# Quantizing two chunks at once, and a reciprocal with Sqrt in place of Ln and Exp, in a fused attention and FP4 feed-forward kernel

## What is computed

```python
xn = _layernorm(x, axis=-1)                      # (x - m) / sqrt(v + 1e-5)
x = x + attention(xn, Wqkv, bqkv, Wproj, bproj, mapping) + ffn(xn, w_gate, w_up, w_down)

def fp4_quant_dequant(x):                        # blocks of 16 along the last dimension
    scale = max(|xb|) / 6.0, at least 1e-12
    idx = searchsorted([0.25, 0.75, 1.25, 1.75, 2.5, 3.5, 5.0], |xb / scale|)
    q = [0, 0.5, 1, 1.5, 2, 3, 4, 6][idx] * sign(xb) * scale

def ffn(x, w_gate, w_up, w_down):                # H = 1024, I = 2816
    gate = fp4_linear(x, w_gate)                 # both operands quantized
    y = fp4_linear(x, w_up)
    h = silu(gate) * y
    return fp4_linear(h, w_down)                 # h is quantized as well
```

## Time and profile before

| | |
|---|---|
| median of 3 runs | 6398.97 us (6398.97 to 6400.04) |
| time of the profiled execution | 6415.45 us |
| span of its slowest core (core 6) | 6413.9 us |
| spans of the 8 cores | 6352.1 to 6413.9 us |
| VectorE busy | 4122.6 us, 64% of the span |
| TensorE busy | 2353.3 us, 37% |
| ScalarE busy | 616.3 us, 10% |
| GpSimd busy | 184.6 us, 3% |

### The profile page before, as it was taken

How to read it: one execution, slowest core, us unless ns; L and a number is a source line. 1 busy time by engine, 2 the same in 40 slices (tenths; PEclk the granted TensorE clock), 3 DMA queues, 4 the chain that set the end, 5 groups by cost and what they waited for, 6 DMA issues and landing times.

```text
span 6413.9 us, 41448 instructions; the slowest of 8 cores (6352.1 to 6413.9 us)
## 1 busy us (share of the span) xinstructions
PE 2353.3 (37%) x12222; PEld 1121.9 (17%) x12373; DVE 4122.6 (64%) x6313; ACT 616.3 (10%) x1270; POOL 184.6 (3%) x249
## 2 busy tenths in 40 slices
PE   2664566646200000002434343434343343433343
PEld 0223422233000000000211111111111111111111
DVE  4882368732799999997565656464646465656565
ACT  0222212221000000000000000000000000000000
POOL 0001100011000000000000000000000000000000
PEclk9775577756555555555656565656666666666666
DMA  4211132112200000000000000000000000000000
GB/s 76 69 59 51 55 118 69 61 45 89 72 29 27 26 26 26 27 24 16 12 9 17 9 17 9 17 9 17 8 17 8 17 8 17 8 17 8 17 8 12
DMA packets 86070, 196.80 MB, mean 31 GB/s; under 512 B 42295, under 2 KB 42311, under 8 KB 85847
## 3 DMA queue, kind: packets, MB, share of 16 engines
q0 software_dynamic: 26544, 100.74, 5.1%
q1 hardware_dynamic: 59304, 93.42, 4.8%
HBM read 135.41 MB, written 67.12 MB: 32 GB/s over the span
## 4 chain that ended last, share of the span: by engine, by line
DVE 30%; PE 10%; issue 7%; DMA 4%; ACT 2%; DVEq 1%; SPq 0%; ACTq 0%; POOLq 0%; POOL 0%
PE psA L926 6%; DVE sc L69 6%; DVE sc L65 6%; DMA sc<-partial_dram 2%; DVE sc L58 2%; DVE sc L60 2%; DVE sc L76 2%; DVE bstats L51 2%; DVE sc L991 2%; DVE sc L71 2%; PE psQ L943 2%; PE psT L917 1%; ACT hqT L961 1%; DMA out<-sc 1%; DVE sc L62 1%
## 5 line engine op out<-in xcount | busy, mean ns | idle before, releaser
L65 DVE SCALAR_TENSOR_TENSOR sc<-sc 128x512 f32<-128x512 f32 (+3 forms) x876 | 734.1, 838 | 94.7 <-DVE sc L65 2.3
L69 DVE SCALAR_TENSOR_TENSOR sc<-sc 128x512 f32<-128x512 f32 (+3 forms) x876 | 734.1, 838 | 93.3 <-DVE sc L69 1.8
L825 PE MATMUL psT<-ident,wq_bf 128*128 128x128 bf16 x528 | 67.1, 307 | 1260.7 <-DVE wq_bf L78 1260.7
L917 PE MATMUL psT<-ident,hq 128*128 128x128 bf16 x704 | 90.3, 306 | 1041.4 <-DVE hq L78 961.5
L982 DVE TENSOR_TENSOR sc<-psA,sc 128x512 f32<-128x512 f32 x32 | 22.1, 692 | 610.8 <-PE psA L926 610.8
L926 PE MATMUL psA<-wdqT,hqT 128*128 128x512 bf16 x1376 | 381.3, 448 | 45.3 <-ACT hqT L961 45.3
L991 DVE TENSOR_TENSOR sc<-sl,psU 128x512 f32<-128x512 f32 x96 | 65.6, 683 | 485.5 <-ACT sl L971 485.5
L825 PEld LDWEIGHTS psT<-ident,wq_bf 128*128 128x128 bf16 x528 | 51.0, 138 | 1276.9 <-issue 1276.9
L60 DVE TENSOR_TENSOR sc<-sc 128x512 f32<-128x512 f32 (+3 forms) x292 | 244.7, 838 | 31.4 <-DVE sc L58 1.4
L71 DVE SCALAR_TENSOR_TENSOR sc<-sc 128x512 f32<-128x512 f32 (+3 forms) x292 | 244.7, 838 | 31.1 <-DVE sc L69 0.9
L76 DVE TENSOR_TENSOR sc<-sc 128x512 f32<-128x512 f32 (+3 forms) x292 | 244.7, 838 | 30.8 <-DVE sc L74 0.5
(11 more groups left out here) (161 smaller groups left out, 4483.1 us busy)
## 6 DMA issues: line engine op xcount, KB each, us to landing
sc<-xin SPq DMA_DIRECT2D x64, 512.0 KB
qkv_dram<-qkv_tile POOLq DMA_DIRECT2D x32, 768.0 KB, 3.6
partial_dram<-sc POOLq DMA_DIRECT2D x32, 512.0 KB, 3.4
sc<-partial_dram SPq DMA_DIRECT2D x32, 512.0 KB
out<-sc POOLq DMA_DIRECT2D x32, 512.0 KB, 2.9
wrow<-wg SPq DMA_DIRECT2D x22, 512.0 KB
wrow<-wu SPq DMA_DIRECT2D x22, 512.0 KB
xqT_dram<-xqTst POOLq DMA_DIRECT2D x32, 256.0 KB, 4.4
```

The lines of the kernel that those rows point to most:

```text
L65: sv.inc(vec.scalar_tensor_tensor(L[:, 0:n], a2[:, 0:n], c, L[:, 0:n], ALU.is_gt, ALU.add))
L69: sv.inc(vec.scalar_tensor_tensor(S[:, 0:n], a2[:, 0:n], c, S[:, 0:n], ALU.is_gt, ALU.add))
L917: m = tensor.transpose(psT[:, 128 * c:128 * (c + 1)], hq2[:, (gt - 1) % 2, 128 * (8 * g + c):128 * (8 * g + c + 1)], ident[:])
```

## The change

Two independent edits.

In the layer-norm stage VectorE computes the reciprocal of variance + 1e-5 itself, and ScalarE takes its square root with one activation in place of two. VectorE's instructions per tile become 26 and ScalarE's 9, and the counts are moved accordingly.

In the FFN stage VectorE takes the six chunks in three pairs. It multiplies both chunks of a pair, side by side into `sc2`, and then quantizes them with one call of `_emit_quant` over 1024 columns (768 for the last pair). The instructions per tile fall from 122 to 65. `hmultv` now names the two multiplies at the head of a pair; the waits of TensorE and ScalarE on it are written as before.

```diff
                     def cva(t):
-                        return svA + 25 * t
+                        return svA + 26 * t
 
                     def csa(t):
-                        return ssA + (10 * t - 8 if t >= 1 else 0)
+                        return ssA + (9 * t - 8 if t >= 1 else 0)
...
                                 sv.inc(vec.tensor_scalar_add(stats[:, 14:15], stats[:, 13:14], 1e-5))
+                                vec.wait_ge(sv.h, sv.v)
+                                sv.inc(vec.reciprocal(stats[:, 15:16], stats[:, 14:15]))
                                 vec.wait_ge(ss.h, rstdv(t))
...
-                                    scal.wait_ge(sv.h, cva(t) + 4)
-                                    ss.inc(scal.activation(stats[:, 15:16], stats[:, 14:15], AF.Ln))
-                                    scal.wait_ge(ss.h, ss.v)
-                                    ss.inc(scal.activation(stats[:, 14:15], stats[:, 15:16], AF.Exp, scale=-0.5))
+                                    scal.wait_ge(sv.h, cva(t) + 5)
+                                    ss.inc(scal.activation(stats[:, 14:15], stats[:, 15:16], AF.Sqrt))
...
             def cvf(gt):
-                return svD + (122 * gt - 2 if gt >= 1 else 0)
+                return svD + (65 * gt - 2 if gt >= 1 else 0)
...
             def hmultv(gt, ci):
-                return cvf(gt) + (2 if gt >= 1 else 0) + 20 * ci + 1
+                pq, k = ci // 2, ci % 2
+                return cvf(gt) + (2 if gt >= 1 else 0) + 21 * pq + k + 1
 
             def quantdonev(gt):
-                return hmultv(gt, 5) + 19
+                return cvf(gt) + (2 if gt >= 1 else 0) + 63
...
-                                for ci, (i0, iw) in enumerate(nic_chunks):
-                                    vec.wait_ge(ss.h, siluv(gt, ci))
-                                    ub = psU if ci % 2 == 0 else psB
-                                    uoff = 0 if ci % 2 == 0 else 512
-                                    sv.inc(vec.tensor_tensor(sc2[:, 0:iw],
-                                                             sl[:, 512 * (ci % 2):512 * (ci % 2) + iw],
-                                                             ub[:, uoff:uoff + iw], ALU.mult))
-                                    _emit_quant(vec, sc2[:, 0:iw], iw // 16, bstats,
+                                for pq in range(3):
+                                    pw = 0
+                                    for k in range(2):
+                                        ci = 2 * pq + k
+                                        i0, iw = nic_chunks[ci]
+                                        vec.wait_ge(ss.h, siluv(gt, ci))
+                                        ub = psU if ci % 2 == 0 else psB
+                                        uoff = 0 if ci % 2 == 0 else 512
+                                        sv.inc(vec.tensor_tensor(sc2[:, pw:pw + iw],
+                                                                 sl[:, 512 * (ci % 2):512 * (ci % 2) + iw],
+                                                                 ub[:, uoff:uoff + iw], ALU.mult))
+                                        pw += iw
+                                    _emit_quant(vec, sc2[:, 0:pw], pw // 16, bstats,
                                                 sc3, sc4, sc5, sc6,
-                                                hq2[:, gt % 2, i0:i0 + iw], sv)
+                                                hq2[:, gt % 2, nic_chunks[2 * pq][0]:nic_chunks[2 * pq][0] + pw], sv)
```

More of the change, by code:

```diff
@@ L354, in sc_off @@
                     def sc_off(t):
-                        return 2 if t <= T - 1 else 0
-                    rstdv = lambda t: csa(t) + 2
+                        return 1 if t <= T - 1 else 0
+                    rstdv = lambda t: csa(t) + 1
                     xnTev = lambda tm1: csa(tm1 + 1) + sc_off(tm1 + 1) + 1
@@ L372, in _ @@
                                 if t >= 2:
-                                    sync.wait_ge(sv.h, cva(t - 2) + 5)
+                                    sync.wait_ge(sv.h, cva(t - 2) + 6)
                                 sync.dma_start(out=xbA[t % 2][:],
@@ L440, in _ @@
                                 if t <= T - 1:
-                                    vwait = cva(t) + 6
+                                    vwait = cva(t) + 7
                                     tensor.wait_ge(sv.h, vwait)
```

## The result

The changed kernel takes 6046.72 us (median of 9 runs, 6037.54 to 6143.07), the kernel before 6399.5 us (10 runs, 6385.18 to 6416.46). The ratio is 0.9448, with a 95% interval of 0.9432 to 0.9465: 353 us faster. The forecast was 6082 us with a range of 6048 to 6122.

A forecast was written before the change was run, and what follows sets the result against it. The prediction took VectorE's quantization on a serial FFN tile loop as the bound: 9.86 us a tile, 316 us over 32, plus 1 us of layer norm, off 6415.45, less 16.5 to the median, gives 6082 us, range 6048 to 6122.

The forecast's parts named there:

- What bounds the kernel: FFN stage: each tile is one serial loop of about 108 us, with VectorE's 72 us of quantization on it full length.
- The price of a call: FFN quantization: 4.2 us a call whatever its width, about 0.22 us an instruction, so each merged pair saves 4.2 us.
- Rival (c): FFN quantization: wide instructions each take twice a narrow one, only gaps are saved; 26 us gain, 6372 us; chance 0.02.
- The rule of 58 cycles of fixed cost: FFN quantization: 60 ns saved for each of 57 instructions, 0.8 us a tile, about 6373 us; the sum went by the rows.
- The new wait: First pair of each FFN tile: second multiply waits for chunk 1's silu, 3.73 us plus 0.10; no cost in later pairs.
- The old stretch: VectorE's FFN tile before: five periods of 12.67 us plus a last chunk of 8.63 us, 71.98 us in all.
- The two gaps at no change: FFN loop: down matmuls, store, load and first gate keep their instructions and order, so no change in cost.
- rival (b): FFN loop: TensorE pieces drift to slow kind, 6178 us, or fast kind, near 6000 us; chance 0.04 each.
- The layer-norm part: Layer-norm stage: one ScalarE step out, a VectorE reciprocal in; between -6 and +2 us, taken as -1 us in all.
- Slower (rival d): FFN pairs 1 and 2: banks come back only after the pair's quantization; +330 us, 6729 us; chance 0.02.

The follow-up runs named there:

- e5: Changed kernel with 8 idle multiplies of 1024 columns a tile put in front of the second pair's quantization; 6426.09 us, ratio 0.9994 to the kernel before.
- e7: Changed kernel, but a tile's load waits for the store of the tile two before it, not the last one; 5696.42 us, ratio 0.8885.
- e12: Changed kernel with the earlier load, the next tile's first four chunks ahead of transposes and down matmuls, adds behind the second pair; 4976.55 us, ratio 0.7753.
- e10: Kernel before, with each quantization of 512 columns done as two of 256; 7124.57 us, ratio 1.1082.
- e2: Kernel before with only the layer-norm edit (reciprocal and Sqrt); 6388.81 us, ratio 1.0006.
- e4: Changed kernel, but TensorE and ScalarE take a pair's banks back only when its quantization has ended; one run, 6643.68 us.
- e9: Changed kernel unaltered, timed again beside the kernel before on another chip; 6085.61 us against 6431.02, ratio 0.9461.

## Why the prediction was wrong by 36 us

The mechanism held; what failed are sizes. Two terms of the sum were mis-sized, the wait for the second silu (3.83 us taken, 3.51 measured) and the old stretch (71.98 us taken, 72.28 measured), and the last step, from the profiled slowest core to the median, carried one core's distance from the others over as if it were fixed. Term by term:

- **What bounds the kernel** held: one serial loop a tile, VectorE's stretch on it one to one. e5 put the length back and lost all of the gain; e7 and e12 took the gaps away as the chain of waits had them.
- **The price of a call**, 4.2 us beside its elements, taken from another stage, held (19.66 us again, 1225 ns again), and e10 confirmed it at a third width with 4.4. Rival (c) falls with the 1225 ns: the wide instructions kept their price in this stage. The rule of 58 cycles of fixed cost in the Trainium skill, VectorE: DVE Perf Modes, section on the TRN2 errata, is decided against by measurement: 0.22 us an instruction with the gap, where 60 ns would give 5.7 us a tile in e10 and 22.1 came. The prediction left out that the same section calls this row too low itself and puts the fixed part near 150 cycles; the 159 ns of the earlier trace rows agree with that.
- **The new wait** was there, once a tile, and nowhere else. Its size is the first term that was off: "I take the middle, 3.73 us, and 0.10 us" makes 3.83, and the measured mean from first to second multiply is 3.51 over the cores (3.43 on a die granted the full clock, 3.64 on the slowest core). The middle was taken from the two kinds of tile of core 6, counted as 14 and 16; the trace has 15 with the second silu 4.20 us or more behind the first, 16 at 3.45 and the first tile at 2.17. On core 2 of the same execution no tile is of the slow kind, on cores 0 and 4 four each. With 0.32 x 32 this is 10 us.
- **The old stretch** is the second term: five periods of 12.67 us, read from one chunk. The mean period is 12.72, because of the holds of some 0.36 us; the stretch was 72.28 and not 71.98, 10 us. The new stretch has such holds too, some 0.15 us a tile, which gives about 5 back. In sum the stretch saves 332 us and not 316.
- **The two gaps at no change** held for the mean core (18.64 and 16.34 to 18.61 and 16.25). What failed is the step from there to the slowest core: "The profiled execution took 6415.45 us, so it becomes ..." takes the slowest core of one execution as the start, one with bursts at 0.81 of the clock, whose gaps were 36 us a tile and not 35, and keeps its distance to the others. That distance was 27 us and became 12: 16 us in the profiled executions. On two other chips the FFN edit alone and the changed kernel gained 342 and 345 us and not 353. This part of the miss is chance and not the change's doing: rival (b), in the fast direction and at a fifth of the size. A gain of 342 would have put the time at 6058 us, inside the range; the 15 us of the two mis-sized terms would have been missed all the same.
- **The layer-norm part** held. The normalization starts 0.93 us after line 388 before and 0.92 after (means of 32 tiles on the slowest core), 0.4 us in all where 1 was taken; e2 shows no change.
- **Slower (rival d)** did not occur, as no wait stands in front of the multiplies of pairs 1 and 2; e4 shows that a late hand-over of the banks would have made the kernel 251 us slower than the one before.

## What to carry to other kernels

Where an engine works through a chain of dependent instructions on a serial loop, count the calls, not the elements: two calls merged save the fixed part of each instruction, and a row of the same helper at the wide width in another stage gives it to 0.1 us. Check then where the merged input is waited for and at which point the buffers go back, for a late hand-over costs more than the merge brings. Take the mean over the tiles and over all cores as the start of a sum, not one tile of the slowest core; and ask first whether the loop has to be serial, as here the order of work (e12, 1109 us) was worth three times the merge (345 us on the same chip).

## What the runs showed of the hardware that was not expected

Beside 0.50 and 1.00 the granted TensorE clock of a burst can be 0.81; 16 matmuls of 512 columns then take 4.20 us and not 3.46, and in the profiled execution of e9 the die with such bursts took 57 us longer than the one without. VectorE has holds of about 0.36 us in front of an instruction that waits for no other engine (0.46 us in place of 0.10 at 4062.88). They are no matter of chance: in the FFN stage of the kernel before all eight cores have the same 29, at the same instructions, and in the changed kernel 15; they lie 68 or 69 VectorE instructions apart or a multiple of that. So they go with the place in the list of instructions. What causes them, no run here shows.
